# GRU recommender on one core: lane 0 alone in halves first, then each lane in turn beside halves of the next

## The reference

```
x  = emb_table[input_ids]                       # [2048, 50, 128]
xp = einsum('bth,hk->btk', x, kernel) + b_i     # k = 384: z, r, candidate
step(h, xt):
    rz, rr, rh = split(h @ rec_kernel + b_r)
    z, r = sigmoid(xz + rz), sigmoid(xr + rr)
    hh   = tanh(xh + r * rh)
    h    = z * h + (1 - z) * hh
logits = h_at_last_position @ emb_table.T       # [2048, 12501]
```

## Time and profile before

| | us |
|---|---|
| median of 3 runs | 1208.89 |
| profiled execution, device time | 1205.95 |
| its span in the trace | 1204.1 |
| PE busy | 1064.9 (88%) |
| PEld busy | 804.9 (67%) |
| DVE busy | 798.4 (66%) |
| POOL busy | 763.7 (63%) |
| ACT busy | 693.7 (58%) |

### The profile page before, as it was taken

One profiled execution on the slowest core, in us unless ns is written; L12 is line 12 of the kernel. 1 busy time (PEld: TensorE's weight loads), 2 busy tenths in 40 slices (PEclk: granted clock), 3 DMA queues, 4 the chain that ended last, 5 costly groups with the idle time before them and its releaser, 6 DMA issues.

```text
span 1204.1 us, 17546 instructions
## 1 busy us (share of the span) xinstructions
PE 1064.9 (88%) x6031; PEld 804.9 (67%) x6031; DVE 798.4 (66%) x1481; ACT 693.7 (58%) x1203; POOL 763.7 (63%) x812
## 2 busy tenths in 40 slices
PE   7968777877777778777899999999999999999997
PEld 6964444444444444444588888888888888888775
DVE  5745555555555555555677777888888887777644
ACT  4443444444444444444477777777777788888543
POOL 0017777777777777777777777777777777663000
PEclk9989999999999999999999999999999999999999
DMA  8986565656565656565588889989899999997799
GB/s 259 350 320 175 167 175 166 176 166 175 167 176 167 175 167 175 166 175 167 169 258 288 290 295 297 297 294 297 291 296 291 296 298 331 310 306 270 257 356 324
DMA packets 127495, 294.29 MB, mean 244 GB/s; under 512 B 18096, under 2 KB 33456, under 8 KB 127408
## 3 DMA queue, kind: packets, MB, share of 16 engines
q0 software_dynamic: 51200, 157.34, 45.3%
q1 hardware_dynamic: 76208, 135.84, 31.2%
HBM read 171.30 MB, written 121.81 MB: 243 GB/s over the span
## 4 chain that ended last, share of the span: by engine, by line
PE 56%; POOL 26%; issue 11%; DMA 5%; DVE 1%; ACT 0%; SPq 0%; DVEq 0%; ACTq 0%
POOL gathered L369 26%; PE x_ps L452 6%; PE x_ps L453 6%; PE x_ps L454 6%; PE r_ps L419 3%; DMA out_dram<-logits 3%; PE c_ps L419 3%; PE r_ps L432 3%; PE z_ps L432 3%; PE z_ps L419 3%; PE r_ps L433 2%; PE r_ps L436 2%; PE c_ps L432 2%; PE c_ps L433 2%; PE c_ps L436 2%
## 5 line engine op out<-in xcount | busy, mean ns | idle before, releaser
L369 POOL DMA_INDIRECT gathered<-gate_table,index x800 | 761.8, 952 | 338.1 <-issue 229.4
L570 ACT ACTIVATE table_rows<-r_ps,zr_bias 128x512 f32<-128x512 f32 (+1 forms) x250 | 151.2, 605 | 200.7 <-PE r_ps L427 162.6
L704 DVE SCALAR_TENSOR_TENSOR c_ps<-c_ps,bias_sb,table_rows 128x512 f32<-128x512 f32 (+1 forms) x250 | 162.8, 651 | 132.1 <-PE c_ps L427 98.6
L572 ACT ACTIVATE z_ps<-z_ps,zr_bias 128x512 f32<-128x512 f32 (+1 forms) x250 | 144.2, 577 | 182.4 <-PE z_ps L427 143.0
L562 ACT ACTIVATE logits<-x_ps,nan_row 128x512 f32<-128x512 f32 (+1 forms) x325 | 214.4, 678 | 42.8 <-PE x_ps L454 27.9
L709 DVE TENSOR_TENSOR table_rows<-z_ps,state 128x512 f32<-128x512 f32 (+1 forms) x250 | 145.0, 580 | 113.6 <-ACT z_ps L572 113.4
L419 PE MATMUL r_ps<-ident,gathered 128*128 128x128 f32 x800 | 107.6, 248 | 119.3 <-issue 107.6
L713 DVE SCALAR_TENSOR_TENSOR c_ps<-z_ps,table_rows 128x512 f32<-128x512 f32 (+1 forms) x250 | 147.7, 591 | 59.8 <-ACT table_rows L579 59.4
L419 PEld LDWEIGHTS r_ps<-ident,gathered 128*128 128x128 f32 x800 | 84.9, 141 | 138.2 <-issue 131.5
L716 DVE TENSOR_TENSOR state<-table_rows,c_ps 128x512 f32<-128x512 f32 (+1 forms) x250 | 145.3, 581 | 26.1
L579 ACT ACTIVATE table_rows<-c_ps,bias_sb 128x512 f32<-128x512 f32 (+1 forms) x250 | 149.7, 599 | 16.2 <-PE c_ps L419 14.7
(11 more groups left out here) (97 smaller groups left out, 1538.8 us busy)
## 6 DMA issues: line engine op xcount, KB each, us to landing
out_dram<-logits SPq DMA_DIRECT2D x192, 512.0 KB, 4.5
gate_table<-table_rows SPq DMA_DIRECT2D x24, 768.0 KB, 5.5
gathered<-gate_table,index POOLq DMA_INDIRECT x800
emb_rows<-in_L_rec_emb_table_dram SPq DMA_DIRECT2D x48, 256.0 KB, 5.8
out_dram<-logits SPq DMA_DIRECT2D x8, 213.0 KB, 3.7
logits<-in_r_input_ids_dram SPq DMA_DIRECT2D x1, 400.0 KB, 4.8
logits<-in_r_input_mask_dram SPq DMA_DIRECT2D x1, 400.0 KB, 6.2
gate_table<-table_rows SPq DMA_DIRECT2D x2, 192.0 KB, 9.3
```

The lines of the kernel that those rows point to most:

```text
L369: nc.gpsimd.indirect_dma_start(tile_rows(slot, n).bitcast(F32), None, table, bass.IndirectOffsetOnAxis(ap=index[:, tile, b.t:b.t + 1], axi ...
L570: nc.scalar.activation(r, r_bank, ACT.Sigmoid, bias=zr_bias[:, 1:2]).then_inc(s_r, 1)
L704: nc.vector.scalar_tensor_tensor(out=c_bank, in0=c_bank, scalar=bias_sb[:, 1, 2:3], in1=r, op0=ALU.add, op1=ALU.mult).then_inc(s_scaled, 1)
```

## The change

The order of the blocks is written anew; no instruction's code changes. There are 325 blocks now. First 50 times the two halves of lane 0 (100 narrow blocks, no pairs, the vocabulary in every fourth). Then 50 times lane 1 wide and a half of lane 2, the halves in turn; each wide block carries a pair. Then 25 times a half of lane 3 and lane 2 wide; each block carries a pair. Last 75 narrow blocks of lane 3, of which two in three carry a pair. These four stretches are called stages 1 to 4. The split into parts begins at block 200, with stage 3, so stage 2 keeps the fp32 matmuls. As before 150 pairs stand beside blocks and 50 behind them, now in groups of one lane each.

```
     lanes = [(lane, 0, LANE) for lane in range(LANES)]      # removed
     a, b = (3, 0, HALF), (3, HALF, HALF)                    # removed
     order = [lanes[0], lanes[1]] * T + [lanes[2], a, lanes[2], b] * (T // 2) + [a, b] * (T - T // 2)   # removed
     return order, 2 * T, lambda g: g >= 2 * T, [range(0, 4), range(4, 6), range(6, 8)]                 # removed
+    def halves(lane):
+        return [(lane, 0, HALF), (lane, HALF, HALF)]
+
+    half = T // 2
+    order = halves(0) * T
+    second = len(order)
+    for i in range(T):
+        order += [(1, 0, LANE), halves(2)[i % 2]]
+    third = len(order)
+    for i in range(T - half):
+        order += [halves(3)[i % 2], (2, 0, LANE)]
+    fourth = len(order)
+    a, b = halves(3)
+    gone = [order.count(h) for h in (a, b)]
+    for i in range(gone[1], T):
+        order += [b, a] if gone[0] + i - gone[1] < T else [b]
+
+    def carries(g):
+        if g < second:
+            return False
+        if g < third:
+            return order[g][2] == LANE
+        return g < fourth or (g - fourth) % 3 != 2
+
+    return order, third, carries, [range(2 * lane, 2 * lane + 2) for lane in range(LANES)]
```

## The result

The changed kernel takes 1214.79 us (median of 6 runs, 1214.04 to 1217.80), the kernel before 1209.65 (6 runs beside them, 1208.09 to 1210.09): a ratio of 1.005, interval 1.0037 to 1.0063. That is 5.1 us slower. The profiled execution of the changed kernel took 1215.07 with a span of 1213.30, which is 9.2 above the span of 1204.10 before. The two profiled executions lie 4 us further apart than the medians do: the one of before took 1205.95, 3.7 under the median of 1209.65, and the one of the changed kernel lies at its median.

A forecast was written before the change was run, and what follows sets the result against it. The old kernel was bound successively by POOL's gathers, PE twice, then stores. New stages end at 341.0, 722, 911.5 and 1129; plus 80.1 makes 1209.1, 5.0 over 1204.1, so median 1214, range 1201 to 1231.

The forecast's parts named there:

- Stage 1: 100 narrow blocks of lane 0: paced by gathers at 2.50 us a block, 250 us, next stage starting at 341.0.
- Stage 2: Wide block with pair plus narrow block: a chain through copies, sigmoid and scale takes 7.58, 379 plus 2 for late gathers.
- The loop of 2.33: Stage 1: DVE's in-order path from one block's scale to the next, 2.33 us; with vocabulary, four blocks take 10.0.
- 131 more: Stage 2 against the old kernel's gather-paced first stretch: 381 us instead of 250 for supposedly the same gathers.
- Stage 3: Lane 3 halves with wide lane 2, all with pairs: 25 iterations of 7.58 us, 189.5, ending at 911.5.
- Stage 4: 75 narrow blocks, 50 with a pair: 219.5 us less 2 for short chunks, ending at 1129.
- The triple: Stage 4: two blocks with pairs at 3.00 us and one without at 2.78, together 8.78.
- the short chunk: First pair of each group of lanes has a short chunk: some 2 us less over stages 3 and 4.
- Behind the blocks: After the last block: the same 50 pairs, paced by the stores, unchanged at 80.1 us.
- From the span to the median: Whole kernel: the 5.0 us difference of profiled spans, added to the old median 1208.89, gives 1213.9.
- Six gathers take 7.50, so B is PE's by a hair: Old kernel's second stretch, 383.2 us: a wide and narrow block take PE 7.58 against 7.50 for their gathers.
- the terms cancel: Rival, whole kernel: stage 2 at 7.50 and all else as forecast, giving 1209 us; chance 16%.

The follow-up runs named there:

- the first two experiments: Changed kernel with stage 2's copies moved behind the narrow block's sigmoids: 1213.41 us; changed kernel with stage 2's pairs on narrow blocks: 1212.44 us.
- the three edits that freed stage 2: Changed kernel with stage 2's copies later (1213.41 us); pairs on narrow blocks (1212.44); the latter plus stage 4's pairless blocks first (one) and last (1200.84).
- the slower kernel: Changed kernel with the split into state parts starting at stage 2 instead of stage 3: 1219.88 us, ratio 1.0114 to the kernel before.

## Why the prediction was right

By its own steps:

- **Stage 1.** Stage 2 was to start at 341.0 and started at 341.60. The loop of 2.33 was met (blocks 2.33 apart). With a vocabulary chunk a block takes 2.87, so the chunk adds 0.54, not 0.7, and four blocks need 9.86, not 10.0. So PE does not run at 2.50 each, as the prediction said one would see: it runs at the loop's pace and now and then waits once for a gather (1.35 us at 243.07). The length is the gathers', as forecast: 25 x 9.86 would be 246.5, and the stage's blocks take 252.4.
- **Stage 2.** 7.60 against 7.58, and every link within 0.03. The length was to be 381 and is 379.96. The copies as the cause were shown from both sides: taken off the path the stage falls to 375.9 and 375.0, and one more adds 0.56 of its 0.63 in each iteration. The copies' price is thus 4 to 5 us above the gathers' floor. It is small because the wide block's state on DVE, which the prediction did not chain, would hold the same scale nearly as long, 0.18 us less. One sign was wrong: POOL was to start waiting for PE in this stage. It did not; the cycle is only 0.10 over the gathers', and PE merely falls behind POOL. The prediction's short form ("131 more" than A "for the same gathers") compares unlike pieces: stage 2 issues 300 gathers, the second half of A 200. The 46 half blocks that get fp32 matmuls anew are 48 in the traces (252 against 204). The sum rests on neither: from 341 to the end of the blocks before took 783.0 us, stages 2 to 4 took 789.85, and 788 were forecast.
- **Stage 3.** 189.10 against 189.5.
- **Stage 4.** 217.5 was said, 220.79 measured. The triple was right: 3.02 + 3.01 + 2.78 = 8.81 against 8.78. What was missed is the first block, 4.31 long, whose units wait 1.83 for lane 2's last state part. The block starts give the rest. The first three blocks take 4.31 + 2.53 + 2.36 = 9.20; less the wait that is 7.37, 1.4 under a triple, which would be the short chunk. The other 24 triples give 24 x 0.04 = 0.9. Over stages 3 and 4 together 407 were forecast and 409.89 came: 1.83 for the wait, 0.9 for the triples, and 0.2, so the 2 us for the short chunks were about right. That the wait for the older block's state sets the third block was shown by putting such blocks together: 2.36 each, and the kernel is faster than before.
- **Behind the blocks.** 81.85 against 80.1. No edit touches this stretch, yet from the start of the last block to the end it takes 80.9 to 84.9 in the seven profiles of the new order named here, so the 1.8 is within what it varies by.
- **From the span to the median.** The spans differ by 9.2, the sum said 5.0; the 4.2 between them are 0.6 of stage 1, -1.0, -0.4 and 3.3 of stages 2 to 4, and 1.8 behind the blocks. The median came out at 1214.8 all the same, because the prediction added the 2.9 us by which the old profiled execution lay below its median, and the new one lies at its median. Two errors of 3 to 4 us met. The place of the loss is shown; that the number agrees to 1 us is partly luck.

One step failed without an effect on the sum: "Six gathers take 7.50, so B is PE's by a hair". The 1.250 was read from A and used for B. The group row of POOL in the kernel before, first 130 to 500 us in A, then 600 to 900 us in B:

```profile
L369 POOL DMA_INDIRECT gathered<-gate_table,index x296 | 279.9, 946 | 90.2 <-issue 90.2
...
L369 POOL DMA_INDIRECT gathered<-gate_table,index x239 | 229.0, 958 | 72.8 <-issue 68.3 <-PE c_ps L419 4.6
```

gives 370.1/296 = 1.250 in A, and in B 301.8/239 = 1.263, 7.58 for six. POOL and PE are equal there, and the trace can't say which of the two bounds B. This is also where the gain of the first two experiments went. Stage 3 takes 189.1 where PE arrives behind POOL (changed kernel; 189.05 with the pairless blocks last, 189.5 with the third copy) and 192.0 to 193.4 where stage 2 ran at the gathers' pace and PE has few gathers in store (four kernels). The store can be measured as the time from a block's last gather issue to the block's start: in stage 3 it is never under 8.0 us in the first three kernels and falls to between 3.3 and 4.1 in the other four. Stages 2 and 3 together took 569.1 us in the changed kernel and 567.0 to 568.4 with the three edits that freed stage 2. The rival "the terms cancel" (1209) had stage 2 at 7.50 and everything else as forecast; when an edit made stage 2 that fast, stage 3 gave 3 us back.

## What to carry to other kernels

Where an engine works through blocks in order, its own load is not the question but what stands in front of the instruction that the next block waits for: two copies on an ACT that is idle 4 tenths of the time set a stage's cycle, because the short block behind them had no work of its own to cover them. What such work costs is the distance to the next path, not its own length: 1.26 us of copies cost 0.10 an iteration, because a path through DVE was 0.18 shorter and the gathers' pace 0.10. Taking work out of every third block brings little when its wait for an older block stays; the same blocks side by side were 0.42 us shorter each. And a stage made faster pays only if the next one has slack: ask what the late stage inherits.

## What the runs showed of the hardware that was not expected

Gathers are a little slower where they meet DVE making the state parts: 1.250 us from one to the next in A and in stage 2 of the changed kernel, 1.263 in B, 1.272 in stage 2 of the kernel that makes parts there. Stage 4 of the changed kernel makes parts as well, but only 3 of its 140 gathers start in a cast, and a gather takes 0.945 on average there as in A.

The parts are two DVE instructions, the cast and the subtraction behind it. The kernel before shows a meeting with each:

```profile
810.01 0.94 POOL L369 DMA_INDIRECT gathered<-gate_table,index  x1 [0.30 <-issue]
...
810.53 0.54 DVE L686 CAST state_hi<-state 128x256 fp32r<-128x256 f32 x1
811.10 0.43 DVE L688 TENSOR_TENSOR state_lo<-state,state_hi 128x256 fp32r<-128x256 f32 x1
811.25 1.09 POOL L369 DMA_INDIRECT gathered<-gate_table,index  x1 [0.30 <-issue]
```

The cast comes second here and takes 0.54 instead of 0.28; then the gather comes second, to the subtraction, and takes 1.09 instead of 0.95. In the eight profiles of undisturbed runs (the two kernels and six experiments), 229 gathers besides the first of each take over 1.0 us, up to 1.20. All of them started inside a cast (121) or inside the subtraction (108), and none of the 3856 that started during any other DVE instruction did. The added time is what was left of the DVE instruction at the gather's start, less 0.13 us: in the timeline of the slower kernel above, 0.42 - 0.13 - 0.13 = 0.16. Of the 291 gathers that started with more than 0.16 us left, 267 fit within 0.03. The other 24 started within 0.03 us of the DVE instruction; they kept their 0.95, and the DVE instruction took some 0.05 longer.

The Trainium skill, "SBUF — State Buffer", section "Who interferes with whom", states that a cast can enter a mode in which DVE holds the port pair that it shares with GpSimd for the whole instruction, and that the issue order decides who blocks. The trace agrees that the cast runs in such a mode as far as its time shows it: 512 elements in 0.42 us, as long as a subtraction takes for 256, 0.42. It agrees on the order as well, by the cast of 0.54 and the gather of 1.09 above. The subtraction is not that fast, 0.42 us for 256 and 0.69 for 512, and lengthens gathers all the same; of DVE's instructions in a block it is the only one that reads both inputs from SBUF, the others have one in PSUM. No run took the cast or the subtraction away alone or put it elsewhere, so this cause is read from the traces and not isolated. In the stage above it is 50 x 6 x (1.272 - 1.250) = 6.6 us, some 5 of them from casts and 1 from subtractions.

Also open is why every kernel ran 16% longer in two rounds of runs. The profile of the changed kernel from there shows a lower granted clock in stages 1 to 4 (0.92, 0.95, 0.97 and 0.99 against 0.99 to 1.00), but that is not all: its stage 2 takes 453.9 us instead of 380.0, and PE is busy for only 23 of the 74 us more (380.2 against 356.9).
